# Eight-core fused transformer kernel: V copies and first int8 transposes moved to ScalarE, softmax sums one step sooner, input LayerNorm of the last stage issued in three parts

## The chip, the cores and the metric

The kernel runs on the 8 cores of one Trainium2 chip. Each core takes one of the 8 sequences (4096 tokens of 1024 values, float32) and runs the same program on it; nothing is exchanged between cores. The metric is the device time of the slowest core in microseconds (us). The engines of a core are named as in the profile: PE is TensorE (PEld its weight loads), DVE is VectorE, ACT is ScalarE, POOL is GpSimd, and SP is SyncE, whose queue starts all the DMAs here.

## The reference

```python
# x: (8, 4096, 1024); _layernorm has no gain or bias
x = x + _layernorm(attn(_layernorm(x), gamma0, w_qkv0, w_out0))       # causal, 8 heads of 128
x = x + _layernorm(int8_matmul(_layernorm(x), rhs))                   # both sides rounded to int8
x = x + _layernorm(attn(_layernorm(x), gamma1, w_qkv1, w_out1))
x = x + _layernorm(qlora_ffn(_layernorm(x), ...))
# attn: x / |x| * sqrt(1024) * gamma -> q, k, v -> softmax(causal(q k^T / sqrt(128))) v -> w_out
# qlora_ffn: h = x; 3 times: y = gelu(layernorm(h @ W0 + b0)); h = h + y @ W1 + b1
#            W = (q / 7.5 - 1) * scale + lora_b @ lora_a, six matrices of 1024 x 1024
```

## The kernel before

Every engine's instructions are issued in the order in which the Python code emits them; a helper for each engine (`PE`, `DV`, `AC`, `GP`, `DMA`) adds an instruction with the tokens that it waits for. There is no scheduler: the place of a call in the code is the place in the engine's queue. The program is five stages one after the other.

1. **Layer 0, projections** (`emit_attn`, first part). Eight chunks C of 512 tokens. Each chunk has 24 groups g of 8 matmuls: g 0 to 7 give K, 8 to 15 give Q, 16 to 23 give V. A group writes one of four PSUM banks, and the next group that uses the bank waits for its copy (`grp_free`): ACT copies K and Q (L625, L633), DVE copies V (L639). DVE also takes the maxima of the squared norms (L603). In the last chunk (C = 7) DVE centres a tile of the output weights behind each V group (`centre_wo`, L573 to L576), and at g = 20 it makes the softmax guard `negM` (`guards`, L582 to L584), on which the first exp waits.
2. **Layer 0, attention** (`emit_attn`, second part). A list of steps (query tile qt, head h, pair of key blocks pr); query tile 0 has two steps for a head. Step i issues exp of step i (ACT, L735), the scores of step i + 2 (PE, L726), the product with V of step i (L752), and on odd pr the sums of the probabilities (L769). At the end of a head `head_end` splits the sums into a bf16 high and low part (`hi`, `lo`, DVE L781 and L782); `totals` adds them on PE (L787, L789), `divide` takes their reciprocal by Ln and Exp on ACT (L794, L796) and multiplies (DVE L797, `feat`). `totals` and `divide` are put into a list `todo` with the step at which they are issued. The sums of the next head wait for `lo`, and `hi` of the next head stands behind `feat` in DVE's queue. `last_tiles` finishes the last query tile; for each token tile it makes the rounded int8 values of the next stage, whose last ACT step is L907.
3. **Int8 stage** (`emit_mid`). For each of 32 token tiles, `Q(t)` transposes the integers on PE and copies them out of PSUM (L1104, tile `m_qT`), `G(t)` multiplies (L1113), and `Y`, `E1`, `E2`, `L1`, `L2`, `T` normalise, add to x and prepare the next layer's input.
4. **Layer 1**, as stages 1 and 2, without the integers; in its projections DVE, ACT and POOL also fold the six weight matrices of the last stage.
5. **Last stage** (`emit_f1`). 48 units of 8 slots (one slot an output block `oc`): 2 batches of 4 token groups (512 tokens each) by 3 blocks. `Y1` units multiply (PE L1328), evict on ACT (L1333), square on POOL (L1338) and sum on PE (L1315, `stat`); their LayerNorm and gelu (`norm` with DVE's reciprocal L1352, `act` with DVE L1358 and ACT L1360) are issued in the slots of the unit behind. `Y2` units multiply (L1373) and add on DVE (L1378). `Y2_last` units make 4 output tiles each (PE L1402 to L1410, DVE L1413 to L1419, ACT L1422, POOL L1426). Six PSUM banks are used in turn. Units 0 to 7 are block 0 of batch 0 (Y1 of groups 0 and 1, Y2 of 0 and 1, Y1 of 2 and 3, Y2 of 2 and 3), 8 to 15 block 1, 16 to 19 the Y1 of block 2, 20 to 23 its Y2_last; 24 to 47 are batch 1, of which 24 is the first Y1.

   The input LayerNorm of token tile t, the prologue, is issued into these units: `pro_stats(t)` is a chain of 11 kinds of small DVE instructions (bn_stats L1282, bn_aggr L1284, an inverse root L215 to L220, L1286), ended by one ACT instruction (L1288, tile `f_prep`) that waits for the chain; behind it the DMA that loads tile t + 2 is issued, which waits for that ACT instruction in SP's queue. `pro_transpose(t)` transposes on PE (L1297) and copies on ACT (L1303). `at(slot, fn)` puts a call into a slot; a negative slot issues it at once, ahead of the units. The bias row of the last matrix (`f_b5f`) is loaded and converted on DVE (L1473, L1474) ahead of all that stands in slots from 0 on.

## Time and profile before

| | |
|---|---|
| Median of 3 runs | 3965.1 us (3794.8 to 4138.7) |
| The profiled execution | 3800.7 us; its span on the slowest core, 4, is 3799.1 us |
| Spans of the 8 cores | 3778.8 to 3799.1 us, granted clock 0.942 to 0.945 |
| Busy share of the span | PE 86%, ACT 56%, DVE 54%, POOL 24% |
| Layer 0 projections | 0 to 479 us |
| Layer 0 attention | 479 to 1342 us |
| Int8 stage | 1342 to 1598 us |
| Layer 1 projections | 1598 to 2046 us |
| Layer 1 attention | 2046 to 2856 us |
| Last stage | 2856 to 3799 us |

The stages are cut where the first matmul of the next one starts on core 4. A busy share is an average over stages with different limits: in the attention stages ACT's exp is nearly always at work, in the last stage PE is. In a row of the timeline the first number is the start in us from the start of the span, the second the time of the instructions merged into the row, and the bracket at the end is the idle time of that engine ahead of the row and what ended it.

### The profile page before, as it was taken

What the parts mean: (1) busy time and instruction counts of PE and PEld (TensorE: products, weight loads), DVE (VectorE), ACT (ScalarE), POOL (GpSimd) and SP (SyncE); (2) the same over time, 40 slices, a digit from 0 to 9 for tenths busy, and PEclk for the clock granted to TensorE, in tenths of its full rate; (3) what the DMA queues carried; (4) which work ended last, traced back from release to release, by engine and by line L of the source; (5) the groups of instructions that cost most, each with busy time, mean ns of one, the idle gap of its engine ahead of it and who ended that gap; (6) DMA issues with size and microseconds to landing.
All of it is one profiled execution on the core that took longest, in us unless ns stands there. A gap on an engine that the chain in (4) does not pass through costs nothing.

```text
span 3799.1 us, 45235 instructions; the slowest of 8 cores (3778.8 to 3799.1 us)
## 1 busy us (share of the span) xinstructions
PE 3264.3 (86%) x16411; PEld 1378.4 (36%) x16736; DVE 2056.3 (54%) x3495; ACT 2143.0 (56%) x2756; POOL 921.4 (24%) x868
## 2 busy tenths in 40 slices
PE   5999868898999867589996899999994899879996
PEld 2444423333333334333332333333332344334442
DVE  5666557664443477555555543322225665775548
ACT  2111147887888646523232788888874563544553
POOL 2333311000110034355553100000001131332333
PEclk9999979999999988899998999999997999989998
DMA  6111212224221467246664221111014200230004
GB/s 206 47 65 56 87 41 95 90 88 70 74 71 42 131 225 243 98 154 173 190 175 137 73 82 62 45 45 45 23 39 158 100 23 23 78 133 1 1 6 161
DMA packets 104287, 347.25 MB, mean 91 GB/s; under 512 B 13632, under 2 KB 17216, under 8 KB 99200
## 3 DMA queue, kind: packets, MB, share of 16 engines
q1 hardware_dynamic: 104064, 344.34, 28.4%
q8 instruction: 132, 2.16, 0.2%
q14 instruction: 91, 0.75, 0.1%
HBM read 237.33 MB, written 106.96 MB: 91 GB/s over the span
## 4 chain that ended last, share of the span: by engine, by line
PE 52%; DVE 23%; ACT 17%; issue 3%; DMA 3%; POOL 1%; SPq 0%; another core or an unknown queue 0%; DVEq 0%; POOLq 0%; ACTq 0%
PE pp L726 9%; PE pp L614 8%; ACT s_probs L735 8%; PE pp L752 8%; PE pp L820 5%; PE pp L619 5%; PE pp L1373 5%; PE pp L1328 4%; PE pp L769 3%; ACT f_yg L1360 2%; DMA s_fsc<-scT 2%; DVE f_r L1352 1%; ACT s_rcp L796 1%; PE pp L598 1%; DVE f_u L1358 1%
## 5 line engine op out<-in xcount | busy, mean ns | idle before, releaser
L735 ACT ACTIVATE s_probs<-pp,s_negM 128x1024 bf16<-128x1024 f32 (+2 forms) x1152 | 1125.6, 1038 | 207.1 <-PE pp L726 199.1
L726 PE MATMUL pp<-s_q,s_kT 128*128 128x512 bf16 (+3 forms) x2215 | 639.2, 368 | 107.2 <-ACT s_probs L735 71.7
L752 PE MATMUL pp<-s_probs,s_v 128*128 128x512 bf16 (+3 forms) x2271 | 646.6, 366 | 12.3 <-POOL s_probs L742 7.0
L742 POOL TENSOR_SCALAR_AFFINE_SELECT s_probs<-s_probs 128x256 bf16<-128x256 bf16 x256 | 114.0, 445 | 1410.9 <-ACT s_probs L735 1365.3
L1328 PE MATMUL pp<-f_h,f_w 128*128 128x512 bf16 x1503 | 360.0, 386 | 5.5 <-ACT f_h L1303 3.4
L1338 POOL TENSOR_TENSOR f_sq<-f_yg 128x512 bf16<-128x512 bf16 x192 | 210.5, 1096 | 529.9 <-ACT f_yg L1333 477.7
L726 PEld LDWEIGHTS pp<-s_q,s_kT 128*128 128x128 bf16 x2304 | 185.9, 99 | 404.2 <-ACT s_probs L735 211.1
L752 PEld LDWEIGHTS pp<-s_probs,s_v 128*128 128x128 bf16 x2304 | 218.9, 99 | 260.0 <-POOL s_probs L742 30.1
L781 DVE CAST s_hi<-pp 128x512 bf16<-128x512 f32 x128 | 88.5, 692 | 316.9 <-PE pp L769 310.4
L625 ACT ACTIVATE s_kT<-pp 128x512 bf16<-128x512 f32 x128 | 76.1, 596 | 324.1 <-PE pp L614 321.7
L1373 PE MATMUL pp<-f_yg,f_w 128*128 128x512 bf16 x1002 | 231.4, 389 | 22.6 <-DVE f_h L1378 12.4
L769 PE MATMUL pp<-s_probs,ones 128*32 128x512 bf16 (+4 forms) x2302 | 240.1, 376 | 5.7 <-DVE s_lo L782 5.3
L820 PE MATMUL pp<-s_wq,s_feat 128*128 128x512 bf16 x876 | 215.8, 388 | 14.6 <-DVE s_feat L797 6.1
L826 DVE BATCH_NORM_STATS2 s_bst<-pp 128x6 f32<-128x512 f32 x112 | 78.3, 699 | 276.3 <-PE pp L820 267.2
L797 DVE TENSOR_TENSOR s_feat<-pp,s_rcp 128x512 bf16<-128x512 f32 x128 | 88.5, 692 | 251.1 <-ACT s_rcp L796 248.8
L1333 ACT ACTIVATE f_yg<-pp,bc 128x512 bf16<-128x512 f32 x192 | 127.6, 679 | 163.0 <-PE pp L1328 158.2
L1328 PEld LDWEIGHTS pp<-f_h,f_w 128*128 128x128 bf16 x1536 | 151.8, 99 | 186.4 <-issue 12.6
L628 POOL TENSOR_TENSOR s_sq<-s_kT 128x512 bf16<-128x512 bf16 x128 | 136.5, 1067 | 258.0 <-ACT s_kT L625 243.9
L633 ACT ACTIVATE s_qst<-pp 128x512 bf16<-128x512 f32 x128 | 75.4, 596 | 210.0 <-PE pp L614 208.6
L1360 ACT ACTIVATE f_yg<-f_u,lbcol,lgcol 128x512 bf16<-128x512 bf16 x192 | 148.7, 809 | 45.9 <-DVE f_u L1358 45.2
L635 POOL TENSOR_TENSOR s_sq<-s_qst 128x512 bf16<-128x512 bf16 x128 | 139.0, 1086 | 144.1 <-ACT s_qst L633 122.8
L1352 DVE RECIPROCAL f_r<-f_r 128x512 f32<-128x512 f32 x24 | 80.5, 3353 | 161.5 <-ACT f_r L1350 161.5
(187 smaller groups left out, 5001.3 us busy)
## 6 DMA issues: line engine op xcount, KB each, us to landing
s_x<-x SPq DMA_DIRECT2D x64, 512.0 KB, 4.4
xbuf<-s_x SPq DMA_DIRECT2D x64, 512.0 KB, 2.7
s_fqi<-qwT SPq DMA_DIRECT2D x48, 512.0 KB, 5.2
s_fsc<-scT SPq DMA_DIRECT2D x48, 512.0 KB
qspill<-s_qst SPq DMA_DIRECT2D x16, 1024.0 KB, 7.2
s_q<-qspill SPq DMA_DIRECT2D x16, 1024.0 KB, 5.7
m_x<-xbuf SPq DMA_DIRECT2D x32, 512.0 KB, 5.4
xbuf<-m_x SPq DMA_DIRECT2D x32, 512.0 KB, 2.8
```

Of the source, the lines that this page charges most:

```text
L614: fn = lambda e, b=b, fi=fi, o=o, wb=wb, xn=xn: e.matmul(pf[b], wb[:, fi, o * 128:(o + 1) * 128], xn[:, fi, :], start=(fi == 0), stop=(fi ...
L619: fn = lambda e, b=b, fi=fi, tt=tt, hf=hf, xn=xn: e.matmul(pf[b], xn[:, fi, tt * 128:(tt + 1) * 128], S.wv[:, fi, hf * 512:(hf + 1) * 512] ...
L635: sq_tok[g] = GP(lambda e, o=o: e.tensor_mul(S.sq[:, o % 4, :], S.qst[:, o, :], S.qst[:, o, :]), ev, sq_free[g % 4])
L726: s_tok[i] = PE(lambda e, kc=kc, q0=q0, c0=c0, b=b, h=h, qt=qt: e.matmul(PS[b][:, c0:c0 + 512 - q0], S.kT[:, h, kc * 128:(kc + 1) * 128], ...
L735: tok = AC(lambda e, b=b, w=w, sl=sl, h=h, qt=qt: e.activation(S.probs[:, sl, 0:w], PS[b][:, 0:w], AF.Exp, bias=S.negM[:, h, qt:qt + 1], s ...
L752: tok = PE(lambda e, kc=kc, q0=q0, c0=c0, sl=sl, h=h, po=po, first=first, last=last: e.matmul(po[:, q0:512], S.v[:, kc, h * 128:(h + 1) * ...
L769: tok = PE(lambda e, out=out, ones=ones, sl=sl, c0=c0, q0=q0, first=first, pr=pr, qt=qt: e.matmul(out, ones, S.probs[:, sl, c0:c0 + 512 - ...
L820: tok = PE(lambda e, fi=fi, tt=tt, hf=hf: e.matmul(MISC, S.feat[:, qt % 2, fi, tt * 128:(tt + 1) * 128], S.wo[:, fi, hf * 512:(hf + 1) * 5 ...
L1328: tok = PE(lambda e, j=j, oc=oc, b=b: e.matmul(pf[b], F.w[i][:, j, oc * 128:(oc + 1) * 128], F.h[hb][:, j, :], start=(j == 0), stop=(j == ...
L1338: sqt.append((k, GP(lambda e, oc=oc, k=k: e.tensor_mul(F.sq[:, k, :], F.yg[yb][:, oc, :], F.yg[yb][:, oc, :]), ev, S["sq_free"][k])))
L1360: g_ready[g] = S["u_free"][n] = AC(lambda e, oc=oc, n=n: e.activation(F.yg[yb][:, oc, :], F.u[:, n, :], AF.Gelu, bias=M.lbcol[:, blk, oc:o ...
L1373: tok = PE(lambda e, j=j, oc=oc, b=b: e.matmul(pf[b], F.w[i][:, j, oc * 128:(oc + 1) * 128], F.yg[yb][:, j, :], start=(j == 0), stop=(j == ...
```

## The change

Four edits.

- In the last chunk of the projections (both layers) ACT copies the 8 V groups (`AF.Copy`) in place of DVE.
- In query tile 0 (both layers) `totals` is issued at step i + 1 instead of i + 2; `divide` stays at i + 2. Later query tiles are as before.
- In the int8 stage `Q(0)` and `Q(1)` are copied out of PSUM by ACT.
- In the last stage `pro_stats` is cut in two: `pro_stats` keeps the DVE chain, and the new `pro_apply` holds the ACT instruction and the load of tile t + 2. `prologue(t, s, apply, stats)` issues the chain at slot s - stats, the ACT instruction at s - apply and the transpose at s. For tiles 4 to 7 the distances are 4 and 2, for later ones 7 and 4. The slots s are as before except for tiles 16 to 23, whose transposes come 3 slots later (71, 79, ... for 68, 76, ...); there the chain stays in its slot (64, 72, ...). For tiles 24 to 31 the chain is issued at 164, 168, ..., 192 and the ACT instruction at 167, 171, ..., 195, where both stood.

```diff
--- before.py
+++ after.py
@@ -636,9 +636,14 @@
                     S.sq[:, o % 4, :], S.qst[:, o, :], S.qst[:, o, :]), ev, sq_free[g % 4])
                 qe = ev
             else:
-                ev = DV(lambda e, o=o, b=b, C=C: e.tensor_copy(
-                    S.v[:, C * 4 + o // 2, (o % 2) * 512:(o % 2 + 1) * 512], pf[b]),
-                    tok, *(cast_all if C else ()))
+                out = S.v[:, C * 4 + o // 2, (o % 2) * 512:(o % 2 + 1) * 512]
+                if C == NQ - 1:
+
+                    ev = AC(lambda e, out=out, b=b: e.activation(out, pf[b], AF.Copy), tok,
+                            *cast_all)
+                else:
+                    ev = DV(lambda e, out=out, b=b: e.tensor_copy(out, pf[b]),
+                            tok, *(cast_all if C else ()))
                 v_last = ev
             grp_free[b] = ev
             if made is None and C == 0 and g < 16:
@@ -969,7 +974,7 @@
             todo.pop(0)[1]()
         if pr == 2 * qt + 1:
             totals, divide = head_end(qt, h, av, rs)
-            todo += [(i + 2, totals), (i + (2 if qt == 0 else 4), divide)]
+            todo += [(i + (1 if qt == 0 else 2), totals), (i + (2 if qt == 0 else 4), divide)]
             todo.sort(key=lambda x: x[0])
         if i > 100 and i % 8 == 4:
             next(more, None)
@@ -1101,8 +1106,12 @@
         F["q"][t % 4] = tok
         if t + 4 < NT:
             load_q(t + 4)
-        qT_tok[t] = F["trq"][i] = DV(lambda e: e.tensor_copy(Z.qT[:, i, :, :], TRQ[i]), tok,
-                                     F["qT"][i])
+        if t < 2:
+
+            ev = AC(lambda e: e.activation(Z.qT[:, i, :, :], TRQ[i], AF.Copy), tok)
+        else:
+            ev = DV(lambda e: e.tensor_copy(Z.qT[:, i, :, :], TRQ[i]), tok, F["qT"][i])
+        qT_tok[t] = F["trq"][i] = ev
 
     g_tok = {}
 
@@ -1268,7 +1277,7 @@
     h_buf = {g: g for g in range(6)}
     h_buf.update({6: 0, 7: 1})
     h_ready, h_used, g_ready, w_ready = {}, {}, {}, {}
-    xp_in, xf_in, prepped = {}, {}, {}
+    xp_in, xf_in, stats, prepped = {}, {}, {}, {}
 
 
     def load_xp(t):
@@ -1283,10 +1292,14 @@
                xp_in[t])
         DV(lambda e: e.bn_aggr(F.mp[:], F.bsp[:]))
         rsqrt_eps(DV, F.mp[:, 1:2], cf[:, 0:1], cf[:, 2:3], cf[:, 3:4], prepped.get(t - 2))
-        d = DV(lambda e: e.scalar_tensor_tensor(cf[:, 1:2], F.mp[:, 0:1], -1.0, cf[:, 0:1],
-                                                ALU.mult, ALU.mult))
+        stats[t] = DV(lambda e: e.scalar_tensor_tensor(cf[:, 1:2], F.mp[:, 0:1], -1.0, cf[:, 0:1],
+                                                       ALU.mult, ALU.mult))
+
+    def pro_apply(t):
+        b, k = t % 2, t % 4
+        xs, cf = F.xp[:, b, :], F.cf[:, b, :]
         prepped[t] = S["xp_free"][b] = AC(lambda e: e.activation(
-            F.prep[:, k, :], xs, AF.Identity, bias=cf[:, 1:2], scale=cf[:, 0:1]), d,
+            F.prep[:, k, :], xs, AF.Identity, bias=cf[:, 1:2], scale=cf[:, 0:1]), stats[t],
             S["prep_free"][k])
         if t + 2 < NT:
             load_xp(t + 2)
@@ -1454,22 +1467,24 @@
         else:
             plan[slot // 8][slot % 8].append(fn)
 
+    def prologue(t, s, apply, stats):
+
+        at(s - stats, lambda: pro_stats(t))
+        at(s - apply, lambda: pro_apply(t))
+        at(s, lambda: pro_transpose(t))
+
     for t in range(4):
-        pro_stats(t)
-        pro_transpose(t)
+        prologue(t, -1, 0, 0)
     for t, s in zip(range(4, 16), (1, 3, 5, 7, 12, 17, 22, 27, 30, 33, 36, 39)):
-        at(s - 4, lambda t=t: pro_stats(t))
-        at(s, lambda t=t: pro_transpose(t))
+        prologue(t, s, *((2, 4) if t < 8 else (4, 7)))
     load_w(1)
     b5_in = DMA(F.b5f[:], brow[5:6, :].broadcast_to([64, D]), "fb5")
     for i, s in ((2, 9), (3, 25), (4, 41), (5, 57)):
         at(s, lambda i=i: load_w(i))
     for t in range(16, 24):
-        at(64 + 8 * (t - 16), lambda t=t: pro_stats(t))
-        at(64 + 8 * (t - 16) + 4, lambda t=t: pro_transpose(t))
+        prologue(t, 71 + 8 * (t - 16), 4, 7)
     for t in range(24, 32):
-        at(171 + 4 * (t - 24) - 4, lambda t=t: pro_stats(t))
-        at(171 + 4 * (t - 24), lambda t=t: pro_transpose(t))
+        prologue(t, 171 + 4 * (t - 24), 4, 7)
     DV(lambda e: e.tensor_copy(F.b5[:], F.b5f[:]), b5_in)
     b5_ok = DV(lambda e: e.tensor_sub(F.b5[32:64, :], F.b5f[32:64, :], F.b5[32:64, :]))
     load_xf(0)
```

Three places show what the engines' queues hold now. The line numbers of the changed kernel are its own (L726 is L731 there, L752 is L757, L769 is L774, L787 and L789 are L792 and L794, L1288 is L1301, L1303 is L1316, L1333 is L1346). First PE in query tile 0, one head, before and then changed (`s_q,s_kT` are scores, `s_probs,s_v` the product with V, `s_probs,ones` the sums, `s_hi` and `s_lo` the totals of the head before):

```order
L752 MATMUL pp<-s_probs,s_v 128x512
L752 MATMUL pp<-s_probs,s_v 128x384
L726 MATMUL pp<-s_q,s_kT 128x256
L726 MATMUL pp<-s_q,s_kT 128x128
L752 MATMUL pp<-s_probs,s_v 128x256
L752 MATMUL pp<-s_probs,s_v 128x128
L769 MATMUL pp<-s_probs,ones_46 128x512
L769 MATMUL pp<-s_probs,ones_46 128x384
L769 MATMUL pp<-s_probs,ones_46 128x256
L769 MATMUL pp<-s_probs,ones_46 128x128
L787 MATMUL pp<-s_hi,s_sel 128x512
L789 MATMUL pp<-s_lo,s_sel 128x512
```

```order
L757 MATMUL pp<-s_probs,s_v 128x512
L757 MATMUL pp<-s_probs,s_v 128x384
L792 MATMUL pp<-s_hi,s_sel 128x512
L794 MATMUL pp<-s_lo,s_sel 128x512
L731 MATMUL pp<-s_q,s_kT 128x256
L731 MATMUL pp<-s_q,s_kT 128x128
L757 MATMUL pp<-s_probs,s_v 128x256
L757 MATMUL pp<-s_probs,s_v 128x128
L774 MATMUL pp<-s_probs,ones_46 128x512
L774 MATMUL pp<-s_probs,ones_46 128x384
L774 MATMUL pp<-s_probs,ones_46 128x256
L774 MATMUL pp<-s_probs,ones_46 128x128
```

The two totals matmuls now stand ahead of the next head's second scores, V product and sums, where they stood behind all of them.

Second ACT at the opening of the last stage, from the copy of tile 3's transpose on (`f_prep` is the normalised tile, `f_yg` an eviction of unit 0, `f_h` the copy of a transpose), before and then changed:

```order
L1303 ACTIVATE f_h_164<-pp 128x8x128
L1288 ACTIVATE f_prep<-f_xp,f_cf 128x1024 x2
L1333 ACTIVATE f_yg_170<-pp,bc 128x512 x2
L1303 ACTIVATE f_h_165<-pp 128x8x128
L1288 ACTIVATE f_prep<-f_xp,f_cf 128x1024
L1333 ACTIVATE f_yg_170<-pp,bc 128x512 x2
```

```order
L1316 ACTIVATE f_h_164<-pp 128x8x128
L1301 ACTIVATE f_prep<-f_xp,f_cf 128x1024
L1346 ACTIVATE f_yg_170<-pp,bc 128x512 x2
L1316 ACTIVATE f_h_165<-pp 128x8x128
L1301 ACTIVATE f_prep<-f_xp,f_cf 128x1024
L1346 ACTIVATE f_yg_170<-pp,bc 128x512 x2
```

Ahead of unit 0's first evictions stands one normalised tile (4) instead of two; tile 5 stands where tile 6 stood, and tile 6 comes two evictions and a copy later. In SP's queue the load of tile 7, which waits for tile 5's ACT instruction, now stands behind the loads of weight matrix 1, of the bias row and of two residual tiles.

Third DVE in the Y2_last units (20 to 23), at the border of two output tiles, before and then changed (`f_rr` is the output LayerNorm's coefficient, `f_bst` its statistics, `f_bsp`, `f_mp`, `f_cf` the input LayerNorm's):

```order
L1419 SCALAR_TENSOR_TENSOR f_rr<-f_mv,f_rr 128x1
L1282 BN_STATS f_bsp<-f_xp 128x6 x2
L1284 BN_AGGR f_mp<-f_bsp 128x2
L215 TENSOR_SCALAR f_cf<-f_mp 128x1
L216 TENSOR_SCALAR f_cf<-f_cf 128x1
L219 SCALAR_TENSOR_TENSOR f_cf<-f_cf 128x1
```

```order
L1432 SCALAR_TENSOR_TENSOR f_rr<-f_mv,f_rr 128x1
L1426 BN_STATS f_bst<-pp 128x6
L1291 BN_STATS f_bsp<-f_xp 128x6 x2
L1293 BN_AGGR f_mp<-f_bsp 128x2
L215 TENSOR_SCALAR f_cf<-f_mp 128x1
L216 TENSOR_SCALAR f_cf<-f_cf 128x1
```

The chain of an input tile stood between two output tiles; it now stands between the two bn_stats halves of one, the second half and the output coefficient behind it.

## Rows read from the trace of the kernel before

**Rows 1.** The page's part 4: shares of the chain that ended last, by engine
```profile
PE 52%; DVE 23%; ACT 17%; issue 3%; DMA 3%; POOL 1%; SPq 0%; another core or an unknown queue 0%; DVEq 0%; POOLq 0%; ACTq 0%
```

**Rows 2.** Timeline, end of layer 0's projections (start us, us, engine line, [idle before])
```profile
455.28 0.60 ACT L633 ACTIVATE s_qst<-pp 128x512 bf16<-128x512 f32 x1 [1.34 <-PE pp L614]
...
473.02 0.69 DVE L639 CAST s_v<-pp 128x512 bf16<-128x512 f32 x1
473.82 1.42 DVE L573 BATCH_NORM_STATS2 s_bst<-s_wost 128x6 f32<-128x512 f32 x2
...
479.07 0.93 PE L726 MATMUL pp<-s_q,s_kT 128*128 128x512 bf16 x2 [6.76 <-DVE s_v L639]
...
489.52 0.69 DVE L781 CAST s_hi<-pp 128x512 bf16<-128x512 f32 x1 [1.24 <-PE pp L769]
```

**Rows 3.** Timeline, end of layer 1's projections
```profile
2055.59 1.48 POOL L742 TENSOR_SCALAR_AFFINE_SELECT s_probs<-s_probs 128x256 bf16<-128x256 bf16 x3 [30.66 <-DVE s_wq L576]
...
2058.73 0.69 DVE L781 CAST s_hi<-pp 128x512 bf16<-128x512 f32 x1 [3.36 <-PE pp L769]
```

**Rows 4.** Timeline, first query tile of layer 0: one head from hi to hi
```profile
494.33 0.69 DVE L781 CAST s_hi<-pp 128x512 bf16<-128x512 f32 x1 [0.17 <-DVE s_feat L797]
...
495.80 0.49 PEld L769 LDWEIGHTS pp<-s_probs,ones 128*128 128x128 bf16 x4 [0.21 <-DVE s_lo L782]
...
496.30 0.10 PEld L787 LDWEIGHTS pp<-s_hi,s_sel 128*128 128x128 bf16 x1
...
499.14 0.69 DVE L781 CAST s_hi<-pp 128x512 bf16<-128x512 f32 x1 [0.17 <-DVE s_feat L797]
```

**Rows 5.** Timeline, start of the int8 stage, and a ScalarE copy of the same shape
```profile
1341.88 1.06 ACT L907 ACTIVATE s_qb<-s_dl 128x1024 bf16<-128x1024 f32 x1 [3.27 <-DVE s_dl L901]
1342.09 1.49 DVE L1104 COPY m_qT<-pp 128x1024 bf16<-128x1024 bf16 x2
...
2867.43 1.02 ACT L1303 ACTIVATE f_h<-pp 128x1024 bf16<-128x1024 bf16 x1 [1.13 <-PE pp L1297]
```

**Rows 6.** Timeline, opening of the last stage
```profile
2882.40 1.24 ACT L1288 ACTIVATE f_prep<-f_xp,f_cf 128x1024 bf16<-128x1024 f32 x1 [1.29 <-DVE f_cf L1286]
...
2886.43 1.24 ACT L1288 ACTIVATE f_prep<-f_xp,f_cf 128x1024 bf16<-128x1024 f32 x1 [2.79 <-DVE f_cf L1286]
...
2888.53 1.78 SPq L205 DMA_DIRECT2D f_b5f<-brow  x1
...
2901.39 0.68 DVE L1473 CAST f_b<-f_b5f 64x1024 bf16<-64x1024 f32 x1 [15.00 <-DMA f_b5f<-brow]
...
2903.43 1.42 DVE L1282 BATCH_NORM_STATS2 f_bsp<-f_xp 128x6 f32<-128x512 f32 x2
...
2907.28 1.24 ACT L1288 ACTIVATE f_prep<-f_xp,f_cf 128x1024 bf16<-128x1024 f32 x1 [17.55 <-DVE f_cf L1286]
...
2910.27 0.61 PE L1315 MATMUL pp<-f_sq,ones 128*128 128x512 bf16 x1 [15.06 <-POOL f_sq L1338]
...
2938.51 1.24 ACT L1288 ACTIVATE f_prep<-f_xp,f_cf 128x1024 bf16<-128x1024 f32 x1 [2.11 <-DVE f_cf L1286]
```

**Rows 7.** Waits, whole span: who <- whom: us in total, times, longest
```profile
ACT f_prep L1288 <- DVE f_cf L1286: 130.2, 30, 17.5
...
PE pp L1297 <- ACT f_prep L1288: 59.3, 12, 17.1
```

**Rows 8.** Timeline of PE in the last stage's middle
```profile
3120.61 0.39 PE L1315 MATMUL pp<-f_sq,ones 128*128 128x512 bf16 x1 [2.21 <-ACT f_r L1350]
...
3161.32 1.03 PE L1297 MATMUL pp<-ident_bf,f_prep 128*128 128x128 bf16 x8 [6.52 <-ACT f_prep L1288]
```

**Rows 9.** Windows: start:end, us, busy PE, PEld, DVE, ACT, POOL, clock, DMA
```profile
3318.00:3348.30 30.30, 21.97 (x122) 10.06 (x122) 26.57 (x74) 10.10 (x12) 9.37 (x4) 0.91 0.49 174
```

**Rows 10.** Timeline, output tiles at the end of the last stage's first half
```profile
3297.99 1.86 DVE L219 SCALAR_TENSOR_TENSOR f_cf<-f_cf 128x1 f32<-128x1 f32 x1
...
3394.33 0.61 PE L1315 MATMUL pp<-f_sq,ones 128*128 128x512 bf16 x1 [7.82 <-POOL f_sq L1338]
```

## The prediction

> **What bounds the kernel now.** I read the spans of the cores first: 3778.8 to 3799.1 us at one clock, so core 4 stands for all. The chain that ended last runs over PE for 52% of its length, DVE for 23% and ACT for 17% [rows 1]: no one engine sets the time, so each edit is worth what the local wait behind it is worth. So I read the list of waits, then the timeline around each edit, and followed each wait to the next thing that is late. Three kinds of wait are touched: at the end of both projections PE stands still until DVE has copied V [rows 2]; in query tile 0 DVE, PE and ACT pass one chain round from head to head [rows 4]; in the last stage ACT waits 130.2 us in 30 waits for the input LayerNorm's coefficients, and PE 59.3 us in 12 waits for the normalised tile [rows 7].
>
> **V copies on ACT.** A cast holds DVE for 0.80 us, start to start (473.02 to 473.82, [rows 2]). DVE has a centring of an output weight tile behind each, so it is the late engine: PE waits 6.76 us for the cast before the first scores. With the copies on ACT, which is idle there and takes 0.60 us for the same shape (L633, [rows 2]), PE and ACT run ahead and DVE's queue becomes the only bound: 8 centrings, the guard, then `hi` of head 0. In layer 0 that queue is shorter by 8 x 0.80 = 6.4 us, of which some 0.5 is lost to waits for norms ahead of the first centring, and the 1.24 us that `hi` waited for PE go too, since PE is ahead now: 6.4 - 0.5 + 1.2 = 7.1 us. In layer 1 GpSimd's first mask waits for the last centring in both kernels (30.66 us idle, ended by `s_wq`, [rows 3]) and `hi` comes 3.1 us behind it; the first cast lay in idle time, so 7 x 0.80 = 5.6, say 5.5 us. Bounds for both together: 10 us (a load of weights comes late) and 14 us. Sum **12.6 us**.
>
> The Trainium skill, page "ScalarE: Activation LUTs", section "Rules for kernel authors", speaks against both moves of copies: simple elementwise work belongs on VectorE, which can be up to about three times as fast for each element. The trace does not bear it out for the float32 V copy (0.60 us on ACT, 0.69 on DVE) and does for the bf16 transposes (1.02 us on ACT, 1.49 for two on DVE, [rows 5]); three times 0.75 would make the first of those 2.2 us and the whole time about 3764.
>
> **Totals one step sooner.** From `hi` to `hi` a head takes 4.81 us (494.33 to 499.14, [rows 4]): hi, lo, the next head's sums, totals, Ln, Exp, feat. `totals` starts 0.50 us behind the sums (495.80 to 496.30). Ahead of them it waits for `lo` alone, and the sums now follow in the shadow of Ln and Exp: some 1.2 us of PE work against about 2.9 us until the next `hi`. Queued behind the waiting totals on PE are the next head's second scores, V product and sums; ACT needs those scores only after Exp and one more exp, some 3 us later. So 0.50 us a head, 8 heads, 2 layers: **8.0 us**. Bounds: 0 (the sums become the late thing, when matmuls run at the lower clock) and 16 (twice 0.50, when they do and the chain still shortens by them).
>
> **First transposed integers on ACT.** The DVE copies start at 1342.09, and the first has ended at about 1342.8. In ACT's queue the new copies stand behind L907 of the last token tile, 1341.88 to 1342.94 [rows 5]; with 1.02 us for a copy the first ends at 1343.96. So this edit does not do what it says: PE starts 1.0 us later, and the stage's chain behind it takes that over. **-1.0 us** (bounds -1.1, and +1 if DVE's freed 1.49 us counted).
>
> **Opening of the last stage.** SP issues the loads of weights 1 and of the bias row behind the load of tile 7, which waits for tile 5's ACT instruction (end 2887.67); now they stand behind tile 4's (end 2883.64), 4.0 us sooner [rows 6]. The bias row landed 12.8 us after its issue, DVE waited 15.00 us for it, and tile 6's chain stands behind it in DVE's queue. Before, ACT sat 17.55 us in front of tile 6's instruction with two finished banks' evictions behind it, and PE 15.06 us until 2910.27. Now those evictions come first, and PE waits only for tile 6's transposed input: 2907.28 - 4.0 + 1.24 = 2904.5, against 2910.3, less half a microsecond lost behind: **5.2 us** (bounds 4 and 6).
>
> **Units 1 to 13.** A chain takes 3.85 us of DVE (2903.43 to 2907.28). Tile 9's now stands in slot 10, between the reciprocal of unit 0's LayerNorm and its first multiply, so all gelus that unit 2 waits for move 3.85 us; before it stood in slot 13 and cost ACT 2.11 us (2938.51, [rows 6]). **-1.75 us** (bounds -3.9 and 0). In the Y1 units 4, 10 and 11 ACT held evictions back while it waited for a chain (4.3 us on average, [rows 7]); of this PE shows 2.21 us at 3120.61 [rows 8], and as much again in slots just before and behind it. I take 3 us each for units 10 and 11, which have a gelu backlog, and 1.5 for unit 4: **7.5 us** (bounds 2 and 9; ACT has its own work, so not the whole wait comes back). In unit 13 PE waited 6.52 us for tile 21 [rows 8]; its transpose now comes 3 slots later, and PE has two free banks to fill meanwhile: **5.2 us** (bounds 0 and 6.5).
>
> **Units 20 to 24.** Here PE waits some 33 us, most of it for normalised tiles, but DVE is the bound: 26.57 us busy in 30.30 [rows 9], the rest hand-overs. The work of DVE does not change, so these waits turn into waits for free banks. Two small things change. An L219 step of the chain took 1.86 us instead of 0.22, since GpSimd's add of the output tile (2.34 us) was running [rows 10]; one bn_stats of 0.75 us now comes first, so each of 7 chains stands 0.7 us less, 5 us in all. But the last output coefficient now comes behind the last chain, not ahead of it, which gives back some 5.4 us of it; what is left is that ACT no longer waits for tile 30's chain before unit 24's evictions. ACT reaches these 2.4 us sooner, and PE, idle 7.82 us before 3394.33, with it: **2.4 us** (bounds -4 and 12). Batch 1 has no prologue and stays.
>
> **Sum.** 12.6 + 8.0 - 1.0 + 5.2 - 1.75 + 7.5 + 5.2 + 2.4 = 38.2 us. The profiled execution took 3800.7 us, so **3763 us**, 1.0% less. The median of the three runs shown is 3965.1; the profiled one lies by the lowest, 3794.8, and my number is for a run like these. All low ends together give a gain of 7 us, all high ends 64.
>
> **Rivals.**
> - *The last stage gives only its opening.* DVE and ACT stay as late in units 4 to 24, since their work is the same. For: the busy shares in units 20 to 24 [rows 9]. Against: ACT's waits in units 10, 11 and 13 end with work that is there much sooner. 12.6 + 8.0 - 1.0 + 3.4 = 23 us, 3778 us. Chance 0.2.
> - *PE's waits for normalised tiles come back whole.* If hand-overs, not DVE's work, made the 15 us for a pair of output tiles, units 20 to 24 give some 25 us instead of 2.4: 3740 us. Against: DVE's rows follow one another without a gap. Chance 0.12.
> - *Slower.* The chain now stands ahead of DVE work that others wait for, at 11 places (tiles 9, 11, 12, 13 and 24 to 30): 11 x 3.85 = 42 us if none of it is covered, more than the 38 gained: 3805 us. It decides from the point where PE has less than one filled output tile in front of DVE; against it, PE is busy 21.97 us for four tiles and DVE 26.57 [rows 9]. Chance 0.04.
>
> **How the numbers follow.** My forecast, 3750 to 3775 us, has 0.62; the three rivals 0.36; 0.02 is left for more than 60 us. The range 3740 to 3788 takes in the first two rivals and leaves out some 0.15. A measurement of this kernel tells about 2% (76 us) from no change. No case reaches 76 us of gain except unknown ones (0.03), and the slower one ends at 0.1%; with something unforeseen behind it I give slower 0.03, within 2% 0.94.
>
> **What would show it.** Right: the first scores of layer 0 start before 473 us, `hi` of head 0 at about 482.4 behind the last centring; heads in query tile 0 at 4.3 us where they took 4.8; G(0) of the int8 stage starts one copy, 1.0 us, behind L907's end; the load of the bias row is issued next to tile 4's ACT instruction, and unit 1 starts some 5 us sooner; unit 2 does not gain on unit 1; no wait of PE for `f_prep` in unit 13; units 21 to 23 each still take about 29 us. Wrong: `hi` of heads 1 to 7 waiting for PE's sums; units 21 to 23 at 22 us, as DVE was then not the bound; or longer than 31 us, as PE was then not ahead.

## The result, and the profile after

The changed kernel takes 3732.8 us (median of 4 runs, 3730.3 to 3733.8). Its ratio to the kernel before is 0.983 with a 95% interval of 0.9806 to 0.9854. (In some executions the cores of one die run at a lower clock and take longer; the ratios leave those executions out, and the readings of a trace those cores.) The profiled execution took 3730.3 us where that of before took 3800.7. The gain is about 65 us by the ratio and 70 by the two profiled executions; the forecast was 38, to 3763, and its range ended at 3740. The direction was right and the size was not: the time lies below the range, and the ratio's interval within the 2% that the forecast called its likeliest outcome.

To see where the difference lies I read the same marks in both traces on all 8 cores (the last copy of Q, the first `hi`, the `hi` that opens query tile 1, the first product of each stage and unit) and took the mean over the cores. This table is worked out from the records; the other tables below are made in the same way.

| stretch (us, mean of the 8 cores) | before | after | gain | forecast |
|---|---|---|---|---|
| last Q copy to `hi` of head 0, layer 0 | 34.23 | 26.95 | 7.3 | 7.1 |
| the same, layer 1 | 38.87 | 33.89 | 5.0 | 5.5 |
| query tile 0: `hi` of head 0 to the first `hi` of query tile 1, layer 0 | 52.70 | 38.68 | 14.0 | 4.0 |
| the same, layer 1 | 53.36 | 38.12 | 15.2 | 4.0 |
| last out-projection to the first int8 product | 19.49 | 20.31 | -0.8 | -1.0 |
| last stage, units 0 to 24 | 520.90 | 501.79 | 19.1 | 18.55 |
| layer 0 up to the last Q copy (not changed) | 453.09 | 451.63 | 1.5 | 0 |
| layer 1, first product to the last Q copy (not changed) | 418.54 | 414.27 | 4.3 | 0 |
| all the rest | | | 0.6 | 0 |
| whole span | 3789.9 | 3723.8 | 66.2 | 38.2 |

One term is wrong, query tile 0, by 21 us; 5.8 us lie in stretches that the change does not touch; the others hold to about half a microsecond in all.

The head of the changed kernel's page, on its slowest core, against [rows 1]: PE is 53% of the chain that ended last now, 52% then. No other engine has taken its place.

```profile
span 3728.7 us, 45201 instructions; the slowest of 8 cores (3715.8 to 3728.7 us)
PE 3236.0 (87%) x16411; PEld 1370.5 (37%) x16736; DVE 2037.0 (55%) x3477; ACT 2153.8 (58%) x2774; POOL 921.9 (25%) x868
PE 53%; DVE 23%; ACT 17%; issue 3%; DMA 3%; POOL 1%; another core or an unknown queue 0%; DVEq 0%; SPq 0%; POOLq 0%; ACTq 0%
```

**Query tile 0 after.** The timeline of core 4 (start, busy time, engine, line, tiles; in brackets the idle time ahead), one head from `hi` to `hi`, to be laid beside [rows 4]. In this timeline and those below, rows that the reading does not need are left out.

```profile
488.68 0.69 DVE L786 CAST s_hi<-pp 128x512 bf16<-128x512 f32 x1
488.80 0.55 PE L731 MATMUL pp<-s_q,s_kT 128*128 128x512 bf16 x2 [1.37 <-ACT s_probs L740]
489.36 0.54 PE L757 MATMUL pp<-s_probs,s_v 128*128 128x512 bf16 x2
489.40 0.69 DVE L787 TENSOR_TENSOR s_lo<-pp,s_hi 128x512 bf16<-128x512 f32 x1
490.15 0.39 PE L792 MATMUL pp<-s_hi,s_sel 128*128 128x512 bf16 x1 [0.25 <-DVE s_lo L787]
490.37 0.38 PE L794 MATMUL pp<-s_lo,s_sel 128*128 128x512 bf16 x1
490.85 0.60 ACT L799 ACTIVATE s_rcp<-pp 128x512 f32<-128x512 f32 x1 [1.64 <-PE pp L794]
490.92 0.71 PE L774 MATMUL pp<-s_probs,ones 128*128 128x512 bf16 x4
491.48 0.63 ACT L801 ACTIVATE s_rcp<-s_rcp 128x512 f32<-128x512 f32 x1
492.14 0.69 DVE L802 TENSOR_TENSOR s_feat<-pp,s_rcp 128x512 bf16<-128x512 f32 x1 [2.05 <-ACT s_rcp L801]
492.94 0.69 DVE L786 CAST s_hi<-pp 128x512 bf16<-128x512 f32 x1
```

The totals (L792) start behind `lo`, the sums (L774) run in the shadow of Ln, and the head takes 4.26 us. That is what the forecast said of a head. What it did not see is what most heads of the kernel before looked like. Here is a later one of before, on the same core:

```profile
505.46 0.69 DVE L781 CAST s_hi<-pp 128x512 bf16<-128x512 f32 x1 [0.17 <-DVE s_feat L797]
505.51 0.55 PE L726 MATMUL pp<-s_q,s_kT 128*128 128x512 bf16 x2 [2.31 <-ACT s_probs L735]
506.18 0.69 DVE L782 TENSOR_TENSOR s_lo<-pp,s_hi 128x512 bf16<-128x512 f32 x1
507.07 1.27 PE L769 MATMUL pp<-s_probs,ones 128*128 128x512 bf16 x4
508.14 0.63 PE L787 MATMUL pp<-s_hi,s_sel 128*128 128x512 bf16 x1
508.56 0.63 PE L789 MATMUL pp<-s_lo,s_sel 128*128 128x512 bf16 x1
509.29 0.60 ACT L794 ACTIVATE s_rcp<-pp 128x512 f32<-128x512 f32 x1 [3.36 <-PE pp L789]
511.45 0.69 DVE L781 CAST s_hi<-pp 128x512 bf16<-128x512 f32 x1 [0.17 <-DVE s_feat L797]
```

The four sums take 1.27 us here and 0.71 above: this head ran at the lower clock level. `lo` ended at 506.87, the totals came at 508.14, and the head took 5.99 us. The granted clock has two levels in these traces, 1.00 and 0.50; a figure between them is the mean over a stretch that holds both. The windows of before, one for a head of 4.81 us and two for heads at the lower clock level (columns: length, then busy time of PE, PEld, DVE, ACT and POOL, the granted clock, DMA share, GB/s):

```profile
494.33:499.14 4.81, 2.34 (x13) 1.05 (x14) 2.07 (x3) 2.59 (x5) 0.81 (x2) 1.00 0.12 49
505.46:511.45 5.99, 3.67 (x14) 1.54 (x14) 2.07 (x4) 2.59 (x5) 0.81 (x2) 0.72 0.00 0
522.58:529.16 6.58, 4.27 (x14) 1.61 (x14) 2.07 (x3) 2.60 (x5) 0.81 (x2) 0.74 0.01 1
```

DVE and ACT do the same work in all three; the granted clock and PE's time differ. On core 6 of before three heads in a row ran at 0.50 throughout, and took 6.54, 6.54 and 7.18 us. The same two kinds of head after the change, the second at the lower level:

```profile
484.47:488.68 4.21, 2.52 (x13) 1.05 (x14) 2.08 (x4) 2.60 (x6) 0.81 (x2) 1.00 0.22 86
492.94:497.52 4.58, 3.73 (x14) 1.45 (x14) 2.07 (x3) 2.59 (x6) 0.81 (x2) 0.68 0.00 0
```

From one `hi` to the next within query tile 0 there are 7 intervals on each core and layer. On core 4 of before, layer 0, they are 4.81, 4.81, 6.32, 5.99, 4.87, 6.26 and 6.58 us; after, 4.62, 4.21, 4.26, 4.58, 4.26, 4.26 and 4.26. The step from there to the first `hi` of query tile 1 went from 12.48 to 7.98 us. Over all cores and both layers, 4 to 7 of the 7 intervals of before have a mean granted clock under 0.85, and 1 to 4 (mostly one or two) of after.

**The last stage after.** SP issues the load of the bias row at 2836.80, just after tile 4's ACT instruction (2834.70, 1.24 us) has ended; DVE waits 9.94 us for it (15.00 in [rows 6]):

```profile
2834.70 1.24 ACT L1301 ACTIVATE f_prep<-f_xp,f_cf 128x1024 bf16<-128x1024 f32 x1 [1.65 <-DVE f_cf L1295]
2836.80 0.52 SPq L205 DMA_DIRECT2D f_b5f<-brow  x1
2850.02 0.69 DVE L1488 CAST f_b<-f_b5f 64x1024 bf16<-64x1024 f32 x1 [9.94 <-DMA f_b5f<-brow]
2855.91 1.24 ACT L1301 ACTIVATE f_prep<-f_xp,f_cf 128x1024 bf16<-128x1024 f32 x1 [12.06 <-DVE f_cf L1295]
2857.20 1.04 PE L1310 MATMUL pp<-ident_bf,f_prep 128*128 128x128 bf16 x8 [10.53 <-ACT f_prep L1301]
```

From the list of waits on core 4 (total, times, longest), to [rows 7]:

```profile
ACT f_prep L1301 <- DVE f_cf L1295: 50.6, 13, 13.9
PE pp L1310 <- ACT f_prep L1301: 56.7, 12, 17.6
```

ACT's wait fell from 130.2 to 50.6 us, PE's only from 59.3 to 56.7, while the stage became 19 us shorter. PE's rows on core 4 tell why: four waits of 17.55, 2.81, 3.75 and 3.17 us lie ahead of unit 0 in after, with nearly the same lengths in before (17.10, 2.82, 3.70, 3.04); the 10.53 above is what the 15.06 of `stat` in [rows 6] has become, under another name; and the 6.52 us in unit 13 [rows 8] is gone. In units 21 to 24 PE waits as before at each tile, for 2.4 to 3.9 us where it was 2.3 to 7.9. The first and the longest of the last group, in after:

```profile
2818.12 1.03 PE L1310 MATMUL pp<-ident_bf,f_prep 128*128 128x128 bf16 x8 [17.55 <-ACT f_prep L1301]
3235.75 1.04 PE L1310 MATMUL pp<-ident_bf,f_prep 128*128 128x128 bf16 x8 [3.86 <-ACT f_prep L1301]
```

### The profile page after: what moved, and what is told of

It reads as the page before. It is cut to its first block, busy times and chain, and to the rows that moved or that the text cites. A ratio compares the mean times of both kernels' runs of the same rounds, so it can differ in the third digit from the quotient of the medians.

```text
span 3728.7 us, 45201 instructions; the slowest of 8 cores (3715.8 to 3728.7 us)
## 1 busy us (share of the span) xinstructions
PE 3236.0 (87%) x16411; PEld 1370.5 (37%) x16736; DVE 2037.0 (55%) x3477; ACT 2153.8 (58%) x2774; POOL 921.9 (25%) x868
## 3 DMA queue, kind: packets, MB, share of 16 engines
q1 hardware_dynamic: 104064, 344.34, 29.3%
## 4 chain that ended last, share of the span: by engine, by line
PE 53%; DVE 23%; ACT 17%; issue 3%; DMA 3%; POOL 1%; another core or an unknown queue 0%; DVEq 0%; SPq 0%; POOLq 0%; ACTq 0%
PE pp L731 9%; PE pp L614 8%; ACT s_probs L740 8%; PE pp L757 8%; PE pp L1386 5%; PE pp L619 5%; PE pp L825 5%; PE pp L1341 4%; PE pp L774 3%; ACT f_yg L1373 2%; DMA s_fsc<-scT 1%; DVE f_r L1365 1%; PE pp L598 1%; ACT s_rcp L801 1%; DVE f_rr L219 1%
## 5 line engine op out<-in xcount | busy, mean ns | idle before, releaser
L731 PE MATMUL pp<-s_q,s_kT 128*128 128x512 bf16 (+3 forms) x2214 | 635.1, 366 | 81.0 <-ACT s_probs L740 65.0
L757 PE MATMUL pp<-s_probs,s_v 128*128 128x512 bf16 (+3 forms) x2272 | 642.6, 364 | 13.1 <-POOL s_probs L747 8.4
L731 PEld LDWEIGHTS pp<-s_q,s_kT 128*128 128x128 bf16 x2304 | 185.1, 98 | 369.7 <-ACT s_probs L740 197.7
L757 PEld LDWEIGHTS pp<-s_probs,s_v 128*128 128x128 bf16 x2304 | 217.7, 98 | 259.3 <-POOL s_probs L747 31.5
L774 PE MATMUL pp<-s_probs,ones 128*32 128x512 bf16 (+4 forms) x2302 | 237.1, 374 | 5.0 <-DVE s_lo L787 4.7
L1346 ACT ACTIVATE f_yg<-pp,bc 128x512 bf16<-128x512 f32 x192 | 128.6, 680 | 172.9 <-PE pp L1341 167.9
L1371 DVE TENSOR_TENSOR f_u<-f_yg,f_r 128x512 bf16<-128x512 bf16 x192 | 151.7, 790 | 33.3 <-ACT f_yg L1373 21.8
```

The costliest lines, as they stand in the source:

```text
L731: s_tok[i] = PE(lambda e, kc=kc, q0=q0, c0=c0, b=b, h=h, qt=qt: e.matmul(PS[b][:, c0:c0 + 512 - q0], S.kT[:, h, kc * 128:(kc + 1) * 128], ...
L757: tok = PE(lambda e, kc=kc, q0=q0, c0=c0, sl=sl, h=h, po=po, first=first, last=last: e.matmul(po[:, q0:512], S.v[:, kc, h * 128:(h + 1) * ...
L774: tok = PE(lambda e, out=out, ones=ones, sl=sl, c0=c0, q0=q0, first=first, pr=pr, qt=qt: e.matmul(out, ones, S.probs[:, sl, c0:c0 + 512 - ...
L1371: d = DV(lambda e, oc=oc, n=n: e.tensor_mul(F.u[:, n, :], F.yg[yb][:, oc, :], rs), S["u_free"][n])
```

## The experiments

A ratio is against the kernel before on the same chip. Where none is given (the filler kernels, the totals ahead of the sums, and the last stage in pieces), the marks are laid beside those of the two profiled executions above. A "head" is again an interval from `hi` to `hi`, and "the eight heads" run from `hi` of head 0 to the first `hi` of query tile 1.

**Each edit alone.** The first three kernels are the kernel before with one edit each. The first:

```diff
-            todo += [(i + 2, totals), (i + (2 if qt == 0 else 4), divide)]
+            todo += [(i + (1 if qt == 0 else 2), totals), (i + (2 if qt == 0 else 4), divide)]
```

> The kernel before with one edit: the totals of query tile 0 are issued at step i + 1. Theory 1 (this edit was the mis-sized term): the eight heads from `hi` of head 0 to `hi` of head 8 take about 38.5 us in each layer where they took 52.7 and 53.4 (means of the 8 cores), so this edit alone gives some 29 us, 3772 us beside 3800. Rival (my forecast's size stands, and the rest came from the other edits acting together, V copies that make PE earlier): the eight heads take 48.7 us, 8 us in all, and the slow heads of about 6.3 us stay. In both, the projections from the last Q copy to `hi` of head 0 keep their 34.23 us in layer 0.

Measured: ratio 0.9913 (0.9895 to 0.9931), 3764.5 us. The eight heads take 37.91 and 38.29 us, and the stretch from the last Q copy to `hi` keeps its 34.22. So this edit alone gives about 30 us by the marks; theory 1 holds, and the size in my forecast falls.

The second (the rest of the hunk, marked by dots, keeps DVE's copy for the other chunks):

```diff
-                ev = DV(lambda e, o=o, b=b, C=C: e.tensor_copy(
...
+                if C == NQ - 1:
+
+                    ev = AC(lambda e, out=out, b=b: e.activation(out, pf[b], AF.Copy), tok,
+                            *cast_all)
...
```

> The kernel before with one edit: ACT copies the V groups of the last chunk. Theory 1: from the last Q copy to `hi` of head 0 it takes 26.95 us in layer 0 (34.23 before) and about 33.9 in layer 1 (38.87 before), 12.3 us together, and the eight heads of query tile 0 keep their 52.7 and 53.4 us: about 3788 us. Rival: the earlier and denser PE raises the clock in query tile 0 also without the new place of the totals; then the heads shorten here too, by 10 us or more in a layer, and the time is below 3775.

Measured: ratio 0.9966 (0.9953 to 0.9978). The stretches up to `hi` take 26.95 and 33.78 us, which is 12.4 us less. The eight heads take 53.00 us in layer 0, as before, and 55.89 in layer 1, where before took 53.36. Theory 1 holds for the stretches and for layer 0; the 2.5 us more in layer 1 it did not have. They come with more heads at the lower level: 48 of layer 1's 56 intervals take 5.7 us or more, 43 in before. So an earlier PE does not raise the clock in query tile 0.

The third has the last stage of after: `prologue` with its distances, and `load_w(1)` and the bias row issued earlier by it.

> The kernel before with the last stage of after (the input LayerNorm in three parts, the early bias row) and nothing else. Theory 1: it gives the 18 us that the last stage gained between the two traces, of which 5.1 in its opening, 6.3 in units 10 and 11, 6.0 in units 12 and 13, 3.7 in units 21 to 24: about 3782 us, and all stages ahead are unchanged within 3 us. Rival: part of the 18 us came from the loads of this stage falling into a calmer time; then the opening gains under 3 us here and the sum is 13 us or less.

Measured: ratio 0.9951 (0.9934 to 0.9969), 19 us. Units 0 to 24 take 501.19 us (520.90): unit 0 gives 5.3, units 10 and 11 6.3, units 12 and 13 6.4, units 21 to 24 3.0. Theory 1 holds, and the three edits add up: 33, 13 and 19 us by the ratios, 65 together, as the whole change (each ratio is good to some 5 to 7 us; by the marks the three are 29.9, 12.4 and 19.7).

The fourth is the kernel after without its third edit:

```diff
-        if t < 2:
-
-            ev = AC(lambda e: e.activation(Z.qT[:, i, :, :], TRQ[i], AF.Copy), tok)
-        else:
-            ev = DV(lambda e: e.tensor_copy(Z.qT[:, i, :, :], TRQ[i]), tok, F["qT"][i])
-        qT_tok[t] = F["trq"][i] = ev
+        qT_tok[t] = F["trq"][i] = DV(lambda e: e.tensor_copy(Z.qT[:, i, :, :], TRQ[i]), tok,
+                                     F["qT"][i])
```

> The kernel after without one edit: DVE copies the first two transposed integer tiles, as before. Theory 1: the first product of the int8 stage starts 0.8 us sooner behind the last out-projection (19.5 us, where after takes 20.3), and the time is 1 us below after's, not to be told from it. Rival: ACT's 0.4 us shorter copy pays somewhere in the stage; then its length to the first projection of layer 1 (254.4 us) grows by 1 to 2 us.

Measured: ratio 0.9842 (0.9821 to 0.9863), not to be told from after's 0.983. The first int8 product comes 19.23 us behind the last out-projection (20.31 after), and from there to layer 1 it takes 254.29 (254.44). So the edit costs 1.1 us by the marks and gives nothing back. In the trace of after one sees the copy wait in ACT's queue behind the last integers:

```profile
1315.07 1.06 ACT L912 ACTIVATE s_qb<-s_dl 128x1024 bf16<-128x1024 f32 x1 [3.26 <-DVE s_dl L906]
1316.03 1.92 ACT L1111 ACTIVATE m_qT<-pp 128x1024 bf16<-128x1024 bf16 x2
1317.40 4.95 PE L1122 MATMUL pp<-m_w,m_qT 128*128 128x512 bf16 x15 [18.53 <-ACT m_qT L1111]
```

**Clock or order.** In query tile 0 two things differ between the traces: where the totals stand, and how many heads ran at the lower level. The next kernels tell them apart. The first leaves the order of before and gives PE more to do: behind each head's Ln, four products whose result is overwritten, in time in which PE waited.

```diff
             l = st["misc"] = AC(lambda e: e.activation(S.rcp[:, k, :], MISC, AF.Ln), st["tot", k],
                                 po_free[k], A_mm)
+            if qt == 0:
+                for n in range(4):
+                    PE(lambda e: e.matmul(MISC, M.ones128[:], S.kT[:, 0, 0:512], start=True, stop=True,
+                                          skip_group_check=True), *((l,) if n == 0 else ()))
```

> The kernel before (totals at step i + 2, V copies on DVE) with more work for PE in query tile 0: behind each head's Ln, PE runs four more 128x512 products into the bank that Ln has read; their results are overwritten. It tells the clock from the order. Theory 2 (order): the head cycle is short in after because PE's scores, products and sums no longer stand between `lo` and the totals; here they still do, so where PE runs at the higher level a head takes the 4.81 us of before, and where at the lower one 6 us or more. Even if all heads run at the higher level the eight take no less than 45 us (38 in after). Rival (clock): what mattered is that PE ran at the higher level; then with the filler the eight heads come near 40 us. If the filler does not raise the granted clock, it says nothing on that, and the eight heads stay at 52 to 55 us.

Measured: 3778.2 us in one execution, 22 less than the profiled execution of before, with 64 more products to make. The eight heads take 42.73 and 42.98 us. All 7 intervals of layer 0 are between 4.81 and 4.99 us on every core, at a granted clock of 0.96 to 1.00. In layer 1 only the first interval lies lower, at 0.79 to 0.94 (4.81 to 5.39 us); the last takes 5.33 us at 1.00. The window of core 4 over query tile 0, and one head in it (L798 is the filler):

```profile
486.00:520.00 34.00, 24.47 (x125) 9.57 (x126) 14.42 (x22) 18.28 (x28) 4.88 (x12) 1.00 0.25 73
```

```profile
501.28 0.72 PE L769 MATMUL pp<-s_probs,ones 128*128 128x512 bf16 x4
501.84 0.38 PE L787 MATMUL pp<-s_hi,s_sel 128*128 128x512 bf16 x1
502.05 0.38 PE L789 MATMUL pp<-s_lo,s_sel 128*128 128x512 bf16 x1
503.18 1.04 PE L798 MATMUL pp<-s_kT,ones 128*128 128x512 bf16 x4 [0.75 <-ACT s_rcp L794]
504.68 0.69 DVE L781 CAST s_hi<-pp 128x512 bf16<-128x512 f32 x1 [0.17 <-DVE s_feat L801]
504.74 0.55 PE L726 MATMUL pp<-s_q,s_kT 128*128 128x512 bf16 x2 [0.52 <-ACT s_probs L735]
```

The clock is 1.00 throughout this window, and PE idles 0.75 and 0.52 us a head where it idled 2.3 in one piece. Neither expectation was right in its number. A head keeps its 4.81 us, as theory 2 said, but the eight take 42.7, not 45 or more, because the step into query tile 1 takes 8.6 us (granted clock 1.00) and not 12.5 (0.59 in before): it too was long by the clock. So the lower level alone cost 10.0 and 10.4 us in the two layers, and the order, with the clock held high, is worth 42.73 - 38.68 = 4.1 and 42.98 - 38.12 = 4.9 us.

The same kernel with half the filler (`range(2)` in the edit above):

> e5_filler with two more products for each head in place of four. Theory (the granted clock follows what PE does): with half the filler some heads fall to the lower level again, and the eight heads take 43 to 53 us, between e5_filler (42.7 and 43.0) and before (52.7 and 53.4); fast heads still 4.8 us. Rival (any product in the idle time keeps the clock): 42.7 us again.

Measured: 45.47 and 45.04 us (3773.7 us in its fastest execution). Most other heads still take 4.81 to 4.88 us (the last of the 7 intervals 4.98 and 5.33), and 0 to 2 of the 7 intervals of a core and layer lie at 5.7 us or more, where before had 4 to 6. The theory holds: with less filler more heads fall to the lower level, and with none most do.

Next, the totals at the step of before but ahead of its sums:

```diff
+        if qt == 0 and todo and todo[0][0] <= i:
+            todo.pop(0)[1]()
         if pr % 2 == 1:
             rs = emit_RS(i, [ready[i - 1], ready[i]])
```

> The kernel before with the totals of query tile 0 still at step i + 2, but ahead of that step's sums, where after has them at step i + 1. My forecast priced only this: 0.50 us a head. Theory 2: at the higher clock a head takes 4.3 us here, as in after; at the lower clock the scores and products of step i + 2 (about 1.1 us behind the exp) still stand ahead of the totals, so a slow head takes about 5.2 us against 4.3 to 4.6 in after and 6.3 in before; eight heads 40 to 44 us. Rival (the step does not matter, only the sums): the same 38 us as after at either level.

Measured, on cores 4 to 7: 40.7 us in layer 0 and 40.8 in layer 1. Heads at the higher level take 4.20 to 4.26 us, at the lower 4.5 to 6.0, often as a pair of 4.6 and 5.47; there are 0 to 3 of them on a core and layer. So for a head at the higher level only the place ahead of the sums counts, as the forecast had it. The eight heads take 2.0 and 2.7 us more than in after. Some 1.0 us of that in each layer stands at the higher level too, in the last interval (4.44 us, 4.26 in after) and the step into query tile 1 (8.8, 7.98 in after); the rest comes from the heads at the lower level, where the earlier step counts. A low-clock head of core 4 shows why: the totals (L787) stand behind two products and two scores that the slow clock stretches.

```profile
504.31 0.93 PE L726 MATMUL pp<-s_q,s_kT 128*128 128x512 bf16 x2 [1.24 <-ACT s_probs L735]
505.03 0.95 PE L752 MATMUL pp<-s_probs,s_v 128*128 128x512 bf16 x2
505.78 0.53 PE L726 MATMUL pp<-s_q,s_kT 128*128 128x256 bf16 x2
506.10 0.53 PE L752 MATMUL pp<-s_probs,s_v 128*128 128x256 bf16 x2
506.42 0.63 PE L787 MATMUL pp<-s_hi,s_sel 128*128 128x512 bf16 x1
```

**The last stage in pieces.** Both kernels start from after with DVE's integers (`e4_dve_ints`, e4 in the table below) and put one group of tiles back; each was timed once. First tiles 24 to 31:

```diff
-        prologue(t, 171 + 4 * (t - 24), 4, 7)
+        prologue(t, 171 + 4 * (t - 24), 4, 4)
```

> The kernel after, with DVE copying the first two integer tiles, and with the chains of tiles 24 to 31 back in the slot of their ACT instruction (164, 168, ... ahead of it become 167, 171, ...). Theory 3 (a chain issued away from the slot of the output coefficients is shorter, and ACT finds its coefficients ready): units 22 and 23 take 30.3 and 30.0 us as in before, where e4 had 28.3 and 28.7, and the time is 3.6 us above e4's. Rival (the 3.6 us came from the loads or from PE being ahead): units 22 and 23 stay at 28.3 and 28.7.

Measured: units 22 and 23 take 30.30 and 29.99 us, as before, and units 21 to 24 together 125.2 where e4 took 121.5. Theory 3 holds: 3.7 us. On core 4 the chains of tiles 25 to 30 take 5.39 us here and in before, and 4.59 in after. (The slowest core alone would not have shown it, 3738.7 us against 3736.3 and 3739.1; the mean span is 4.0 us above e4's.)

Then tiles 16 to 23:

```diff
-        prologue(t, 71 + 8 * (t - 16), 4, 7)
+        prologue(t, 68 + 8 * (t - 16), 4, 4)
```

> The kernel after, with DVE copying the first two integer tiles, and with tiles 16 to 23 as in before: transposes in slots 68, 76, ..., chain and ACT instruction four slots ahead. Theory 3: units 12 and 13 go back from 17.5 and 14.3 us to 15.2 and 23.0, units 10 and 11 from 17.3 and 17.7 to 20.9 and 20.4, and so 12.3 us more in all. Rival (units 10 and 11 gained by the earlier chains of tiles 12 to 15, whose change stays here, or by PE being ahead): only units 12 and 13 go back, and it is 6.4 us more.

Measured, in us:

| unit | before | e8 | e4 | after |
|---|---|---|---|---|
| 10 | 20.89 | 19.20 | 17.31 | 17.31 |
| 11 | 20.35 | 20.35 | 17.65 | 17.65 |
| 12 | 15.20 | 16.89 | 17.53 | 17.90 |
| 13 | 22.96 | 23.47 | 14.26 | 14.26 |

Units 10 to 13 take 79.9 us, where e4 took 66.8 and before 79.4. Theory 3 holds in the main, with 13.1 us for its 12.3. Unit 10 goes back only half way, so 1.7 us of its gain belong to the other tiles, as the rival had it for the whole.

**A version that should beat both.** The kernel after, with DVE's integers, tile 9's chain back in slot 13, and this:

```diff
-            todo += [(i + (1 if qt == 0 else 2), totals), (i + (2 if qt == 0 else 4), divide)]
+            todo += [(i + (1 if qt == 0 else 2), totals), (i + (2.5 if qt == 0 else 4), divide)]
             todo.sort(key=lambda x: x[0])
+        while todo and todo[0][0] <= i + 0.5:
+            todo.pop(0)[1]()
```

> A version that should beat both: the kernel after with three edits. In query tile 0 `divide` of a head (Ln, Exp, `feat`) is issued behind `hi` and `lo` of the next head, no longer ahead of them; the chain of tile 9 in the last stage goes back to the slot of its ACT instruction; DVE copies the first two integer tiles. Theory: in after, a head's cycle of 4.26 us is one chain, hi, lo, totals, Ln, Exp, feat, that the next `hi` joins only by its place behind `feat` in DVE's queue. With `hi` ahead of `feat` the chain is cut, and the head takes what the busiest engine needs: PE some 3.1 us at the higher clock level (rows of one head: 0.55 + 0.54 + 0.62 + 0.33 + 0.33 + 0.71), ACT 2.7 us. With hand-overs 3.4 us, so the eight heads take 32 to 33 us in each layer where after takes 38.7 and 38.1: 11 us less. Unit 1 of the last stage goes from 24.0 to 22.4 us, 1.6 less, and the stage ahead of the first int8 product is 0.8 us shorter. About 3718 us beside after's 3732. Rival: the product with V two heads on now waits for `feat` (same bank), and the new chain through it is as long as the old: the heads stay at 4.1 to 4.3 us, and the gain on after is 2.5 us.

Measured: ratio 0.9831 (0.9811 to 0.985), the same as after. On cores 0 to 3 the eight heads take 38.7 to 40.3 us in layer 0 and 37.4 to 39.4 in layer 1, and a head 4.16 us. What the heads gain on after's 4.26 is lost in the step into query tile 1, 9.2 us for 7.98. The theory falls and the rival holds: the V product of the head two steps on waits for `feat`, since it writes the same bank, and the totals stand behind it on PE. From core 1:

```profile
491.54 0.69 DVE L802 TENSOR_TENSOR s_feat<-pp,s_rcp 128x512 bf16<-128x512 f32 x1
492.29 0.55 PE L757 MATMUL pp<-s_probs,s_v 128*128 128x512 bf16 x2 [0.32 <-DVE s_feat L802]
492.68 0.38 PE L792 MATMUL pp<-s_hi,s_sel 128*128 128x512 bf16 x1
494.19 0.69 DVE L786 CAST s_hi<-pp 128x512 bf16<-128x512 f32 x1 [1.95 <-PE pp L774]
```

The change once more beside it:

> The kernel after once more, beside e9_late_divide on the same chip: another execution of the stages that the change leaves alone. If the projections of layer 1 (first product to last Q copy) are again at 414 us where the profiled execution of before took 418.5 (means of the 8 cores), they vary by execution or by what stands ahead; over 417 says that it is by execution.

Measured: ratio 0.9868, with a wide interval (0.98 to 0.9936). The stretches that the change touches are those of after within half a microsecond, and the projections of layer 1 took 416.3 us (414.3 in after). That is between the two answers expected. Over the kernels run here this stretch lies between 413.1 and 417.6 us; the profiled execution of before, with 418.5, is above them all.

Since the totals behind the V product were the trouble, the next kernel keeps the edits of `e9_late_divide` and issues the totals ahead of that product:

```diff
+        while todo and todo[0][0] <= i - 0.4:
+            todo.pop(0)[1]()
         av = emit_AV(i, ready[i])
...
-            todo += [(i + (1 if qt == 0 else 2), totals), (i + (2.5 if qt == 0 else 4), divide)]
+            todo += [(i + (0.6 if qt == 0 else 2), totals), (i + (2.5 if qt == 0 else 4), divide)]
```

> e9_late_divide with one more edit: the totals of query tile 0 are issued ahead of the product with V of step i + 1, behind its scores. In e9_late_divide that product waited for `feat`, and the totals stood behind it on PE: feat 0.69, V product 0.55, totals, Ln, Exp, feat made the chain of 4.16 us anew. Theory: with the totals ahead, two heads share the chain feat, V product, scores, V product, sums, hi, lo, totals, Ln, Exp, feat (0.75 + 0.4 + 0.33 + 0.33 + 0.7 + 1.45 + 0.65 + 1.25, some 6 us, 3 us a head), and the busiest engine, PE with 3.1 us, sets the head: 3.3 to 3.5 us, eight heads in 33 us or less where after takes 38.7 and 38.1; 5 us less in each layer, about 3720 us. Rival: the totals make the next scores no later but the V product and the sums later by their 0.6 us, and `hi` waits for those sums: heads of 4.0 us or more, and no gain on e9_late_divide.

Measured: ratio 0.9824 (0.9796 to 0.9852); the three lowest runs are 3721.2, 3723.2 and 3723.7 us, and those of after 3730.3, 3731.9 and 3733.8. The ratio's interval covers after's, so by time alone this is not told from it; the kernel before, too, was faster at its best on this chip (3790.7 us, against 3794.8 beside after). By the marks it is: the eight heads take 36.12 and 34.83 us, a head 3.73 at the higher level, and the mean span is 3713.9 us against 3723.8 and 3724.1 in the two profiled executions of after. Of these 10 us, 5.9 are in query tile 0, 1.6 in unit 1, 1.1 ahead of the int8 stage. The theory's mechanism holds, its 3.3 to 3.5 us a head does not: the V product still waits for `feat`, by 0.19 us, and ACT for PE. One head of core 1:

```profile
491.66 0.69 DVE L786 CAST s_hi<-pp 128x512 bf16<-128x512 f32 x1 [1.52 <-PE pp L774]
493.14 0.39 PE L792 MATMUL pp<-s_hi,s_sel 128*128 128x512 bf16 x1 [0.27 <-DVE s_lo L787]
493.93 0.55 PE L757 MATMUL pp<-s_probs,s_v 128*128 128x512 bf16 x2 [0.19 <-DVE s_feat L802]
495.40 0.69 DVE L786 CAST s_hi<-pp 128x512 bf16<-128x512 f32 x1 [1.52 <-PE pp L774]
```

## Why the prediction was wrong in size

**V copies on ACT (12.6 us forecast, 12.3 measured): right.** The 7.1 us of layer 0 became 7.3 and the 5.5 of layer 1 became 5.0, and the kernel with this edit alone shows the same. The first scores of layer 0 on core 4 start at 467.4, well ahead of 473. `hi` came at 479.85 rather than 482.4, because the last Q copy of that execution was 2.4 us earlier; counted from that copy, `hi` moved by 7.29 us. The prediction's sentence on the Trainium skill, page "ScalarE: Activation LUTs", section "Rules for kernel authors", leaves out that the page gives its factor of about three for bf16; these copies read float32, where the trace has ACT ahead (0.60 us against 0.69).

**Totals one step sooner (8.0 us forecast, 29.3 measured): the step that failed.** The mechanism was right, and its size was taken from one head. "From `hi` to `hi` a head takes 4.81 us" is true of three intervals of seven at most; the others took 5.3 to 7.2 us at the lower clock. I counted 0.50 us for each head and gave 16 us as the upper bound "when they do and the chain still shortens by them"; doubling the 0.50 was the wrong bound. At the lower level all of PE's work behind the exp (scores, products, sums: 505.51 to 508.14, 2.6 us) stood ahead of the totals, not the sums alone: the totals came 1.27 us behind the end of `lo`, where in the head of 4.81 us from 494.33 on they came 0.6 behind (495.74 to 496.35). And I held the clock fixed, while the change moves it: after the change mostly one or two intervals of seven, and at most four, ran at the lower level. The measured parts are 20.4 us for the clock (the filler alone gives them, with the order of before) and 8.9 us for the order at the higher level, which is what the 8.0 had priced. The split depends on which is counted first: with the order of after a head at the lower level costs 0 to 0.7 us more, where with that of before it was 0.5 to 2.2.

The row that would have told it stands in the trace of before: the windows of the low-clock heads above, at 0.72 and 0.74. The prediction's three rivals had nothing about the clock either.

**First integers on ACT (-1.0 us forecast; -0.8 between the traces, -1.1 against e4): right,** by the mechanism given.

**Last stage (18.55 us forecast, 19.1 measured): right in sum and nearly so in its parts.** Opening 5.2 against 5.1; tile 9's chain -1.75 against -1.6; units 4, 10 and 11 7.5 against 1.25 + 3.58 + 2.70 = 7.5, but units 6 and 7 gave back 2.5 of it, which I had not seen; units 12 and 13 5.2 against 8.7 - 2.7 = 6.0; units 21 to 24 2.4 against 3.8; units 2 and 3 gave 0.8 that no term had. That the sum fits so well is partly luck: the gains beyond the forecast cover the 2.5 us of units 6 and 7, whose cause was not sought. Units 22 and 23 take 28.5 and 28.6 us, and on core 4 DVE is busy 24.4 us of 28.4 and 25.0 of 28.7, so DVE is the bound there as claimed. But the forecast had the shorter chain's gain given back by the last output coefficient and put its 2.4 us at unit 24. The runs show 3.3 of the 3.8 us in units 22 and 23, where the chain is shorter, and 0.4 in unit 24. The forecast's "units 21 to 23 each still take about 29 us" was not so of unit 21, which takes some 38 us in both. The rivals on this stage (its opening alone, or all waits come back) fall, and so does the slower one: of the eleven chains issued ahead of other work only tile 9's has a price that a run ties to it (with it back in its old slot, in `e11b_cut_chain`, unit 1 takes 22.4 us as in before, where after takes 24.0).

**The rest.** 5.8 us lie in the projections ahead of the last Q copies. Nothing there changed; the two stretches together take 871.6 us in the profiled execution of before, 865.9 in after's and 866.1 to 870.7 in the others. So some 4 us of the 70 are most likely the luck of the two profiled executions, and the ratio's 65 fits that. Why this stretch varies stays open.

## What to carry to other kernels

Where a chain goes round many times, price the change on all the rounds, not on one: list the intervals, and where they fall into two groups look at the granted clock beside them. A PE that waits in every round may be running at the lower level because it waits, and then time taken out of the wait can pay twice: the round is shorter, and its matmuls are faster. Whether it is the clock is told by one cheap kernel: give PE useless products in its idle time and see if the kernel becomes faster.

## What the runs showed of the hardware

More work made the kernel faster: four 128x512 products a head in query tile 0 (1.04 us of PE) took 22 us off the whole, 20.4 us of it by the marks in query tile 0. In a round of 4.81 us PE had idled 2.3 us in one piece and was busy 2.34 us; after two such rounds on core 4 of before it fell to the lower level, and ran there for a part of 4 to 7 rounds of 7 on every core. With 0.75 and 0.52 us idle it fell in no round of layer 0, and in layer 1 only the first shows the lower level. The Trainium skill, page "TensorE: Matmul & The Clock Gate", section "HAM oscillation — how this bites in real kernels", describes the pattern for waits on DMA: an engine that waits between short bursts falls back to the lower clock and pays it in every burst. This case's traces agree with the pattern, 0.72 and 0.74 in the low-clock heads, with ACT and DVE in the place of the DMA.

The lower level lengthened the chain itself. The PE of a low-clock head was busy 3.67 to 4.27 us instead of 2.34. The step into query tile 1, which has eight out-projection products in it (3.57 us at 535.42 in before, 1.89 after), took 12.5 us in before; with the same order and the clock at 1.00, in the filler kernel, it took 8.6.
